# The last four output projections of an adapter moved among self-attention's first units, in one block

## Chip, cores, metric

One Trainium2 chip, one of its cores. The metric is the device time of one execution in microseconds, the median of several runs.

## The reference, cut

Four sequences (B = 4) of 512 tokens of width 160 pass an adapter and then a transformer block. Everything is float32. The adapter:

```python
query = hidden_states @ Wq                       # 8 heads of 20
hs = mha(query, enc @ Wk, enc @ Wv)              # against 73 context rows
ca_q1 = einsum('btc,th->bch', ca, Wq_ca)[:, indices, :]   # 96 rows, repeated to 512
ca_hs1 = mha(ca_q1, residual, residual)
ca_hs2 = mha(ca_hs1 @ Wq, ca @ Wk_ca, ca @ Wv_ca)         # against 4 tokens
out = (hs + ca_hs2) @ Wout + b_out + residual
```

The transformer block (20 heads of 64):

```python
x = cross_attention(layer_norm(x, g1, be1), layer_norm(x, g1, be1), wq1, wk1, wv1, wo1, bo1) + x
x = cross_attention(layer_norm(x, g2, be2), context, wq2, wk2, wv2, wo2, bo2) + x
return geglu_ff(layer_norm(x, g3, be3), w_ff1, b_ff1, w_ff2, b_ff2) + x
```

## The kernel before

Each engine's program is written out by hand in the order in which it is to run, and semaphores join the engines. `adapter` has a block of its own; it ends with a barrier over all engines. `selfattn`, `crossattn` and `feedfwd` then share a second block, each appending to every engine's queue.

**The adapter** works in units u of 128 tokens: NU = 16, four (QT) to a sequence b. Its loop runs over slots s = 0 to 19, and b, k = divmod(s, 4). In slot s TensorE does `scores1(s)` (the 96 token queries against x, two heads), turns the probabilities of s - 1 (L934), projects out unit s - 7 (`project_out`, L1036 and L1037), makes the scores of unit s - 1 (L1004) and turns unit s - 2's (L1014, L1022). VectorE takes maxima (L1222), subtracts (L1233, L1237), sums and inverts (L1241, L1243), empties the last turned piece (`copy_end`, L1250) and adds projections to x (`update`, L1265). ScalarE takes exponentials (L1122, L1127) and copies (L1114, L1134, L1141). POOL scales by the inverses (L1371, L1375), spreads keys and values over blocks (L1340, L1347), adds the bias (`add_bias`, L1354) and makes the rest of self-attention's split weights (L272, L275). Values times the output weights are folded once per sequence at k = 3 (`fold_values`, L986 and L989) and copied by `copy_folded` (L1259), after `inverses` on VectorE. Turned probabilities, projected queries (L909), folded values and the expanded probabilities of the four tokens (`expand_probs2`, L971) all pass through a ring of two PSUM banks, 2 and 3 (`Turns`): an item waits until the item two before it has been copied out.

Self-attention's first LN (`next_ln`, for sequence 0) is made inside the adapter: statistics at s = 14, `standardize` (L157) at s = 15, `turn` (L165, L172) at s = 17, `scale` (L185, L190) and `round` (L202 to L205) on ScalarE at s = 17, `remainder` (L216, L218) on VectorE at s = 18. Units 13 to 15 are projected out after the loop, unit 12 in slot 19.

SP's queue issues all loads; x_t of sequence 1 is the operand of the queries projection in slot 1, x_pad 0 that of `products1` (L946) in slot 3. POOL wants x in slot 3. After the last weight rest SP issues the `last` loads (later weights).

**Self-attention** works on pairs of heads j = 0 to 9 and units u of four per pair. `project_q`, `project_k` (four matmuls, L228 to L231) and `project_v` (L236 to L239) fill a bank; ScalarE rounds it (`round_q` L491, `round_k` L495) and VectorE makes the rest (`rest_q` L561, `rest_k` L566) or copies v (L571). `scores` (L386) fill two banks; VectorE takes maxima (L575), ScalarE exponentials (L503), VectorE inverses (L579), POOL scales (L647); `turns` (L400), copies (L584, L514) and `pv` (L413) follow. Ahead of the loop over sequences a start-up, written out by hand, does the pairs 0 and 1 and units 0 to 5. Batch 0 then begins with `next_v` for pair 2, a turn, and `next_k` for pair 2, which waits for the copy of v:

```python
def next_k(b, j):
    pe.wait_ge(s_vsb.sem, s_vsb.at(b, j))
    project_k(b, j)
```

Before all this each engine increments the semaphores that carry a credit, seven on TensorE. A single bias addition of POOL (`add_bias(0)`, L654) opens its part.

## Time and profile before

| | |
|---|---|
| median of 3 runs | 1015.6 us (1014.93 to 1016.07) |
| the profiled execution | 1019.83 us |
| its span, first to last instruction | 1018.0 us |
| mean granted TensorE clock | 0.993 of full speed |
| busy: TensorE, VectorE, ScalarE, POOL | 974.7, 683.6, 588.9, 377.5 us |
| adapter, start-up, self-attention, rest | 0 to 145, 147 to 163, 163 to 767, 767 to 1018 us |

The profile is one execution. A busy share is an average over stages; what a stage is worth is read from the gaps of the engine that bounds it, each with the instruction that ended it (its releaser). In a timeline row stand start, duration, engine, line, operation, output and inputs, shapes and count, and in brackets the idle time ahead of it with the releaser; "issue" means that nothing in the core released it. Times in the rows are us from the span's start.

### The profile page before, as it was taken

The page shows a single profiled execution, that of the slowest core. Times are in us where ns is not written, and L with a number is a line of the kernel's source. Part 1 is how long each engine was busy: PE and PEld are TensorE (multiplying, and loading weights), DVE is VectorE, ACT ScalarE, POOL GpSimd, SP SyncE. Part 2 cuts the span into 40 slices and gives each one's busy share as a digit, 9 for nine tenths or more (in the row PEclk, how much of TensorE's full clock was granted, in tenths as well). Part 3 has the DMA queues.
Part 4 walks back from the last instruction along what each step waited for, and adds up shares of the span by engine and source line. Part 5 has one row for each costly group of instructions (what it writes and reads, how often), then busy time and mean ns, then how long its engine had stood idle before and what let it go on. Part 6 is the DMA issues. An engine that isn't in the chain of part 4 may idle for free.

```text
span 1018.0 us, 17405 instructions
## 1 busy us (share of the span) xinstructions
PE 974.7 (96%) x6346; PEld 700.8 (69%) x6346; DVE 683.6 (67%) x1164; ACT 588.9 (58%) x1326; POOL 377.5 (37%) x486
## 2 busy tenths in 40 slices
PE   7999989999999999999999999999999989999998
PEld 3566665666567666567666567666566689998887
DVE  3666737776674776674776674776636879999463
ACT  3665636666764666764666764666735455445442
POOL 3576714443332443332444332434311034444120
PEclk9999999999999999999999999999999999999999
DMA  9310230000000000000000000000001330000000
GB/s 268 102 42 2 55 96 1 1 2 1 1 2 1 1 1 2 1 1 1 1 1 1 2 1 2 1 1 1 2 1 36 104 83 1 1 2 1 2 27 26
DMA packets 19585, 22.18 MB, mean 22 GB/s; under 512 B 1366, under 2 KB 17070, under 8 KB 19502
## 3 DMA queue, kind: packets, MB, share of 16 engines
q1 hardware_dynamic: 19502, 21.09, 7.3%
q8 instruction: 51, 0.84, 0.3%
q14 instruction: 32, 0.26, 0.1%
HBM read 15.83 MB, written 1.31 MB: 17 GB/s over the span
## 4 chain that ended last, share of the span: by engine, by line
PE 66%; DVE 10%; ACT 4%; issue 4%; POOL 1%; DMA 0%; SPq 0%; DVEq 0%; ACTq 0%; POOLq 0%
PE banks L413 13%; PE banks L400 12%; PE banks L386 11%; PE banks L420 4%; PE banks L228 3%; ACT sa_probs L503 3%; PE banks L1626 3%; PE banks L229 2%; PE banks L231 2%; PE banks L230 2%; PE banks L1918 2%; DVE ca_top L1761 2%; PE banks L236 2%; DVE ca_probs L1766 2%; DVE sa_negmax L575 1%
## 5 line engine op out<-in xcount | busy, mean ns | idle before, releaser
L647 POOL TENSOR_SCALAR sa_probs<-sa_probs,sa_inverse 128x512 f32<-128x512 f32 x320 | 217.7, 696 | 362.6 <-DVE sa_inverse L579 362.5
L503 ACT ACTIVATE sa_probs<-banks,sa_negmax 128x512 f32<-128x512 f32 x320 | 215.9, 686 | 125.7 <-DVE sa_negmax L575 125.6
L575 DVE TENSOR_REDUCE sa_negmax<-banks 128x2 f32<-128x1024 f32 x160 | 188.7, 1218 | 10.3 <-PE banks L386 7.3
L400 PEld LDWEIGHTS banks<-ident,sa_probs 128*128 128x128 f32 x1280 | 144.4, 140 | 55.6 <-issue 27.6
L400 PE MATMUL banks<-ident,sa_probs 128*128 128x128 f32 x1280 | 172.5, 275 | 10.0 <-ACT sa_turned L514 5.6
L584 DVE COPY sa_turned<-banks 128x512 f32<-128x512 f32 x160 | 110.2, 688 | 75.3 <-PE banks L400 75.3
L413 PE MATMUL banks<-sa_turned,sa_v 128*64 128x512 f32 x640 | 155.0, 605 | 0.0
L386 PE MATMUL banks<-sa_k_parts,sa_q_parts 64*128 64x512 f32 x960 | 133.1, 408 | 1.9 <-ACT sa_probs L503 1.9
L514 ACT COPY sa_turned<-banks 128x512 f32<-128x512 f32 x160 | 94.3, 589 | 58.1 <-PE banks L400 56.3
L386 PEld LDWEIGHTS banks<-sa_k_parts,sa_q_parts 64*128 64x128 f32 x960 | 84.0, 184 | 30.4 <-issue 14.1
L413 PEld LDWEIGHTS banks<-sa_turned,sa_v 128*64 128x64 f32 x640 | 38.7, 136 | 74.2 <-issue 73.0
L1843 POOL TENSOR_TENSOR ca_probs<-ca_probs,ca_inverse 128x770 f32<-128x770 f32 x32 | 48.2, 1509 | 101.4 <-DVE ca_inverse L1772 101.4
L1626 PE MATMUL banks<-fold_values,ca_turned 119*128 119x160 f32 (+1 forms) x416 | 67.2, 307 | 2.2 <-ACT ca_turned L1705 1.5
L579 DVE RECIPROCAL sa_inverse<-sa_total 128x2 f32<-128x2 f32 x160 | 26.1, 163 | 57.7 <-ACT sa_probs L503 57.7
L503 ACT ACTIVATION_READ_ACCUMULATOR sa_probs<-banks,sa_negmax 128x1 f32 x320 | 64.6, 202 | 0.0
L1626 PEld LDWEIGHTS banks<-fold_values,ca_turned 119*128 119x128 f32 (+1 forms) x416 | 60.8, 196 | 3.6 <-issue 2.8
L1695 ACT ACTIVATE ca_probs<-ca_probs 128x770 f32<-128x770 f32 x32 | 27.0, 847 | 35.6 <-DVE ca_probs L1766 35.6
L1705 ACT COPY ca_turned<-banks 119x512 f32<-119x512 f32 x64 | 30.3, 500 | 28.9 <-PE banks L1614 28.9
L420 PEld LDWEIGHTS banks<-w_o,sa_att 128*128 128x128 f32 x320 | 43.6, 190 | 3.2 <-issue 3.2
L571 DVE COPY sa_v<-banks 128x512 f32<-128x512 f32 x40 | 27.6, 691 | 26.4 <-PE banks L239 26.4
L420 PE MATMUL banks<-w_o,sa_att 128*128 128x160 f32 x320 | 44.5, 300 | 0.0
L1614 PE MATMUL banks<-ident,ca_probs 128*119 128x128 f32 (+1 forms) x208 | 33.4, 281 | 4.4 <-POOL ca_probs L1843 3.6
(205 smaller groups left out, 1701.9 us busy)
## 6 DMA issues: line engine op xcount, KB each, us to landing
ad_x_t<-in_x_turned SPq DMA_DIRECT2D x4, 512.0 KB, 5.0
ad_x_pad<-in_x_padded SPq DMA_DIRECT2D x4, 512.0 KB, 8.8
w_o<-in_L_xattn_wo SPq DMA_DIRECT2D x2, 800.0 KB, 9.0
x<-in_x SPq DMA_DIRECT2D x1, 1280.0 KB, 9.1
out<-x SPq DMA_DIRECT2D x4, 320.0 KB, 2.4
w_q_t<-in_L_xattn_wq_t SPq DMA_DIRECT2D x1, 1120.0 KB, 10.6
fold_values<-ca_turned SPq DMA_DIRECT2D x5, 192.5 KB
fold_values<-ca_probs SPq DMA_DIRECT2D x4, 192.5 KB
```

The lines of the kernel that those rows point to most:

```text
L386: last = pe.matmul(bank[:, e, :], q_parts[rows, j % 2, a, q * P:(q + 1) * P], k_parts[rows, j % 2, c, :], start=(i == 0), stop=(i == 2))
L400: last = pe.transpose(b_turn[e][:, q * P:(q + 1) * P], probs[:, j % 2, e, q, k * P:(k + 1) * P], ident[:])
L413: last = pe.matmul(b_out[e * HD:(e + 1) * HD, :], v[:, V_BUF[j // 2], k, c:c + HD], turned[:, u % 2, e, :], start=(k == 0), stop=(k == QT ...
L420: last = pe.matmul(b_turn[q // 2][:, q % 2 * D:(q % 2 + 1) * D], att[:, j, q * P:(q + 1) * P], w_o[:, j, :], start=(j == 0), stop=(j == NP ...
L503: act.activation(probs[:, j % 2, e, q, :], b_scores[u % 2][:, e, :], ACT.Exp, bias=negmax[:, u % RING, e:e + 1], accum_out=total[:, u % RI ...
L514: act.copy(turned[:, u % 2, 1, :], b_turn[1]).then_inc(s_evac_act.sem, 1)
L575: dve.tensor_reduce(negmax[:, u % RING, :], b_scores[u % 2], AX_X, ALU.max, negate=True).then_inc(s_max.sem, 1)
L584: dve.tensor_copy(turned[:, u % 2, 0, :], b_turn[0]).then_inc(s_evac.sem, 1)
L647: pool.tensor_scalar(probs[:, j % 2, e, q, :], probs[:, j % 2, e, q, :], inverse[:, u % RING, e:e + 1], 1.0, ALU.mult, ALU.mult).then_inc( ...
L1614: last = pe.transpose(bank[0:w, n * P:(n + 1) * P], p[:, c:c + w], ident[:])
L1626: last = pe.matmul(b_out[t % 2][:, 0:D], turned[0:w, i, :], folded.values[0:w, t // QT, i, :], start=(i == 0), stop=(i == folded.TILES - 1))
L1843: pool.tensor_tensor(p, p, inverse[:, t % RING, u, :].unsqueeze(2).broadcast_to([P, HH, SK]), ALU.mult).then_inc(s_norm.sem, 1)
```

## The change

Adapter and self-attention share the one block, so the barrier between them is gone; semaphores and PSUM-bank handovers take its place (`AdapterEnd`), and SBUF tiles are allocated in another order so that what self-attention writes first does not lie on what the adapter still reads. The expansion for sequence 3 and the output projections of units 12 to 15, with their updates, become functions that self-attention's start-up calls: the expansion ahead of the first scores, two projections ahead of q of pair 2, two at its end. The start-up's order changes on every engine, and k 0 to q 0 use other banks. In the adapter, the LN turn goes to slot 16, `scale` ahead of the last exponential, `round` and `remainder` to slot 17 in two parts each; `copy_folded` is split around `inverses`, in every sequence; on SP's queue x_t of sequence 1 comes ahead of x_pad 0, and x behind the first weight set. POOL waits for the later biases ahead of its first addition.

```diff
+            adapter_end.weights_split(pe)
             ln.ready(pe, 0)
-            project_q(0, 0, b_proj)
+            project_q(0, 0, b_scores[0][:, 0, :])
             project_k(0, 0, b_out)
+            adapter_end.main_updated(pe)
             project_q(0, 1, b_turn[0])
+            adapter_end.expand_probabilities()
+            scores(0, 0)
             project_k(0, 1, b_turn[1])
-            scores(0, 0)
+            adapter_end.expanded(pe)
             scores(0, 1)
             project_v(0, 0, b_proj)
             pe.wait_ge(s_klo.sem, s_klo.at(0, 0))
             project_v(0, 1, b_out)
             for u in range(2, 2 * LEAD):
                 scores(0, u)
+            pe.wait_ge(s_klo.sem, s_klo.at(0, 1))
+            adapter_end.project_first_half()
             project_q(0, 2, b_turn[0])
             for u in range(2 * LEAD, 2 * LEAD + 2):
                 scores(0, u)
+            adapter_end.project_second_half()
             pe.wait_ge(s_qlo.sem, s_qlo.at(0, 2))
+            adapter_end.updated(pe)
+            adapter_end.later_weights_loaded(pe)
...
-            round_q(0, 0, b_proj)
+            round_q(0, 0, b_scores[0][:, 0, :])
             round_k(0, 0, b_out)
             round_q(0, 1, b_turn[0])
+            adapter_end.copy_expanded()
+            exps(0, 0)
             round_k(0, 1, b_turn[1])
-            exps(0, 0)
             exps(0, 1)
             exps(0, 2)
+            exps(0, 3)
             round_q(0, 2, b_turn[0])
-            exps(0, 3)
...
-            rest_q(0, 0, b_proj)
+            rest_q(0, 0, b_scores[0][:, 0, :])
             rest_k(0, 0, b_out)
             rest_q(0, 1, b_turn[0])
-            rest_k(0, 1, b_turn[1])
             maxima(0, 0)
             maxima(0, 1)
+            rest_k(0, 1, b_turn[1])
+            inverses(0, 0)
             copy_v(0, 0, b_proj)
-            copy_v(0, 1, b_out)
-            inverses(0, 0)
             maxima(0, 2)
             inverses(0, 1)
+            copy_v(0, 1, b_out)
             maxima(0, 3)
+            inverses(0, 2)
+            adapter_end.update_first_half()
+            inverses(0, 3)
             rest_q(0, 2, b_turn[0])
-            inverses(0, 2)
-            inverses(0, 3)
+            adapter_end.update_second_half()
...
+            adapter_end.biases_loaded(pool)
             add_bias(0)
...
+        END = NU - QT
+        out_of = lambda u: b_out[:, OUT:OUT + D] if u < END else banks[5][:, (u - END) % 2 * D:((u - END) % 2 + 1) * D]
...
-        block = ctx.enter_context(nc.Block())
+        end = AdapterEnd(weights_split=lambda eng: eng.wait_ge(s_rest.sem, s_rest.at(len(chunks) - 1, 1)),
+                         main_updated=lambda eng: eng.wait_ge(s_x.sem, s_x.at(END - 1, 0)),
+                         expanded=lambda eng: ring.wait_copied(eng, ("expanded", B - 1, 0)),
+                         updated=lambda eng: eng.wait_ge(s_x.sem, s_x.at(NU - 1, 0)),
+                         biases_loaded=lambda eng: eng.wait_ge(s_later, 16 * len(later)),
+                         later_weights_loaded=lambda eng: eng.wait_ge(s_last, 16 * len(last)))
...
             sp.dma_start(ident[:], t["ident"]).then_inc(s_ident, 16)
+            turned_x(1)
             padded_x(0)
             sp.dma_start(flat(wo[:]), t["wo_padded"]).then_inc(s_wo, 16)
             sp.dma_start(b_o[:], w("b_out").unsqueeze(0).broadcast_to([P, D])).then_inc(s_wo, 16)
             sp.dma_start(expand[:], t["expand"]).then_inc(s_wo, 16)
+            split_weights(0)
             sp.dma_start(x[:], tiles).then_inc(s_x_in, 16)
-            split_weights(0)
-            turned_x(1)
             split_weights(1)
             padded_x(1)
             split_weights(2)
...
-                if 1 <= u < NU - 3:
+                if 1 <= u < END:
                     pe.wait_ge(s_x.sem, s_x.at(u - 1, 0))
-                if u == NU - 1:
-                    pe.wait_ge(s_x.sem, s_x.at(NU - QT, 0))
+                if u >= END + 2:
...
-                if s == NU + 2:
-                    expand_probs2(B - 1)
-                if 0 <= s - OUT_LAG < NU - 3:
+                if 0 <= s - OUT_LAG < END:
                     project_out(s - OUT_LAG)
                 if 0 <= u < NU:
                     scores(u)
+                if s == NU:
+                    pe.wait_ge(s_exp1.sem, s_exp1.at(NU - 1, 1))
+                    next_ln.turn(pe, 0, ident, banks[0:2], lambda i: None)
                 if 0 <= u - 1 < NU:
                     turn_probs(u - 1)
                 if k == 0 and 1 <= b <= B:
...
                     fold_values(b)
                 if k == 3 and b + 1 < B:
                     project_queries(b + 1, 1)
-                if s == NU + 1:
-                    pe.wait_ge(s_exp1.sem, s_exp1.at(NU - 1, 1))
-                    next_ln.turn(pe, 0, ident, banks[0:2], lambda i: None)
-            for u in range(NU - 3, NU):
-                project_out(u)
+
+            def project_first_half():
+                project_out(END)
+                project_out(END + 1)
+
+            def project_second_half():
+                project_out(END + 2)
+                project_out(END + 3)
+
+            end.on_tensor(lambda: expand_probs2(B - 1), project_first_half, project_second_half)
...
+                if s == NU:
+                    act.wait_ge(s_later, 16 * len(later))
+                    next_ln.scale(act, 0, banks[0:2])
+                    exp(NU - 1)
+                if s == NU + 1:
+                    next_ln.round(act, 0, lambda eng: None)
                 if k == 2 and 1 <= b < B:
                     exp2(b - 1)
                 if 1 <= s < NU:
...
                     copy_q2(b - 1)
                 if 0 <= u - 1 < NU:
                     copy_turned(u - 1)
-                if 0 <= u < NU:
+                if 0 <= u < NU - 1:
                     exp(u)
                 if s in chunks:
                     i, c = chunks[s]
...
                     copy_queries(b + 1, 1)
                 if s == NU + 1:
                     exp2(B - 1)
-                    act.wait_ge(s_later, 16 * len(later))
-                    next_ln.scale(act, 0, banks[0:2])
-                    copy_expanded(B - 1)
-                    next_ln.round(act, 0, lambda eng: None)
+            end.on_scalar(lambda: copy_expanded(B - 1))
...
-            def copy_folded(b):
-                if b >= 2:
+            def copy_folded(b, half):
+                if b >= 2 and half == 0:
                     dve.wait_ge(s_o.sem, s_o.at((b - 2) * QT + QT - 1, 0))
-                for half in range(2):
-                    item = ("folded", b, half)
-                    ring.wait_made(dve, item)
-                    n = min(3, CH - 3 * half)
-                    dve.tensor_copy(flat(folded[:, b % 2, 3 * half:3 * half + n, :]), ring.bank(banks, item)[:, 0:n * D]).then_inc(ring.s_dve, 1)
+                item = ("folded", b, half)
+                ring.wait_made(dve, item)
+                n = min(3, CH - 3 * half)
+                dve.tensor_copy(flat(folded[:, b % 2, 3 * half:3 * half + n, :]), ring.bank(banks, item)[:, 0:n * D]).then_inc(ring.s_dve, 1)
 
             def update(u):
                 dve.wait_ge(s_o.sem, s_o.at(u, 0))
...
                     shift2(b - 1)
                 if 1 <= s < NU:
                     max1(s)
+                if s == NU + 1:
+                    next_ln.remainder_main(dve, 0, lambda eng: None)
                 if k == 2 and 1 <= b <= B:
                     finish2(b - 1)
-                if 0 <= s - OUT_LAG < NU - 3:
+                if 0 <= s - OUT_LAG < END:
                     update(s - OUT_LAG)
+                if s == NU + 1:
+                    next_ln.remainder_tail(dve, 0)
                 if 0 <= u < NU:
                     shift(u)
                 if s < NU:
                     inverses1(s)
                 if 0 <= u - 1 < NU:
                     copy_end(u - 1)
+                if k == 3 and b < B:
+                    copy_folded(b, 0)
                 if 0 <= u < NU:
                     inverses(u)
                 if k == 3 and b < B:
-                    copy_folded(b)
+                    copy_folded(b, 1)
                 if s == NU - 2:
                     dve.wait_ge(s_x.sem, s_x.at(QT - 1, 0))
                     next_ln.statistics(dve, 0)
                 if s == NU - 1:
                     next_ln.standardize(dve, 0)
-                if s == NU + 2:
-                    next_ln.remainder(dve, 0, lambda eng: None)
-            for u in range(NU - 3, NU):
-                update(u)
+
+            def update_first_half():
+                dve.wait_ge(s_o.sem, s_o.at(END + 1, 0))
+                update(END)
+                update(END + 1)
+
+            def update_second_half():
+                dve.wait_ge(s_o.sem, s_o.at(END + 3, 0))
+                update(END + 2)
+                update(END + 3)
+
+            end.on_vector(update_first_half, update_second_half)
...
-            adapter(nc, t, x, ident, ctx_t, banks, [(w("wq1"), wa), (w("wk1"), wb), (w("wv1"), wc)], raws, later, last, ln1)
             block = ctx.enter_context(nc.Block())
-            x_ready = selfattn(nc, block, x, ident, ln1, ln2, wa, wb, wc, w_o1, bias["bo1"], banks)
+            end = adapter(nc, block, ctx, t, x, ident, ctx_t, banks, [(w("wq1"), wa), (w("wk1"), wb), (w("wv1"), wc)], raws, later, last, ln1)
+            x_ready = selfattn(nc, block, end, x, ident, ln1, ln2, wa, wb, wc, w_o1, bias["bo1"], banks)
```

## Rows read from the trace of the kernel before

**Rows 1.** The page, busy time of each engine over the span
```profile
PE 974.7 (96%) x6346; PEld 700.8 (69%) x6346; DVE 683.6 (67%) x1164; ACT 588.9 (58%) x1326; POOL 377.5 (37%) x486
```

**Rows 2.** By stretch: busy us (count) of each engine, granted clock, DMA share, GB/s
```profile
22.00:26.00 4.00, 4.00 (x8) 1.16 (x8) 0.00 (x0) 0.47 (x1) 1.82 (x2) 0.57 1.03 240
...
148.00:152.00 4.00, 4.00 (x12) 3.11 (x11) 1.38 (x2) 1.64 (x3) 0.00 (x0) 0.57 0.00 0
...
156.00:160.00 4.00, 3.32 (x19) 1.80 (x18) 3.80 (x7) 3.02 (x9) 2.22 (x4) 1.00 0.00 0
...
170.00:180.00 10.00, 10.00 (x66) 6.40 (x63) 7.20 (x12) 7.98 (x21) 4.07 (x6) 1.00 0.00 0
```

**Rows 3.** Timeline of TensorE in the head: start, us, ..., [idle before <-releaser]
```profile
16.91 1.18 PE L1004 MATMUL banks<-ad_k_diag,ad_q_t 128*128 128x292 f32 x4
21.92 3.58 PE L909 MATMUL banks<-ad_x_t,ad_wq 128*128 128x512 f32 x4 [3.83 <-issue]
...
37.15 1.95 PE L909 MATMUL banks<-ad_x_t,ad_wq 128*128 128x512 f32 x4 [0.86 <-DVE ad_folded L1259]
```

**Rows 4.** Timeline of SP's DMA queue, the issue of x_t of sequence 1
```profile
13.30 0.42 SPq L855 DMA_DIRECT2D ad_x_t<-in_x_turned  x1
```

**Rows 5.** DMA issues at 13.3, 4.7 and 6.6: size, us from issue to landing
```profile
ad_x_t<-in_x_turned SPq DMA_DIRECT2D x1, 512.0 KB, 8.5
...
ad_x_pad<-in_x_padded SPq DMA_DIRECT2D x1, 512.0 KB, 5.4
...
x<-in_x SPq DMA_DIRECT2D x1, 1280.0 KB, 9.1
```

**Rows 6.** Waits of 24 to 125 us: total, times, longest
```profile
PE banks L909 <- DVE ad_folded L1259: 3.2, 3, 1.2
```

**Rows 7.** Timeline of VectorE around the first waits and around one fold
```profile
21.24 0.20 DVE L1243 RECIPROCAL ad_inverse<-ad_total 128x8 f32<-128x8 f32 x1
26.60 1.22 DVE L1222 TENSOR_REDUCE ad_negmax<-banks 96x2 f32<-96x1024 f32 x1 [5.16 <-PE banks L924]
...
93.63 0.76 DVE L1241 TENSOR_REDUCE ad_total<-ad_probs 128x8 f32<-128x584 f32 x1 [0.50 <-ACT ad_probs L1127]
...
94.55 1.01 DVE L1259 COPY ad_folded<-banks 128x480 f32<-128x480 f32 x2
98.35 1.22 DVE L1222 TENSOR_REDUCE ad_negmax<-banks 96x2 f32<-96x1024 f32 x1 [2.78 <-PE banks L924]
```

**Rows 8.** Timeline of TensorE, from slot 16 to the start-up of self-attention
```profile
125.38 0.92 PE L934 MATMUL banks<-ident,ad_probs 96*128 96x96 f32 x8 [1.20 <-DVE ad_folded L1259]
...
147.13 0.47 PE L228 MATMUL banks<-ln_y_hi,wa_hi 128*128 128x512 f32 x1 [2.05 <-issue]
...
147.66 0.39 PE L230 MATMUL banks<-ln_y_hi,wa_lo 128*128 128x512 f32 x1
...
150.02 0.63 PE L229 MATMUL banks<-ln_y_lo,wa_hi 128*128 128x512 f32 x1
```

**Rows 9.** Timelines of VectorE and TensorE, maxima 4 and k of pair 2
```profile
162.30 2.33 DVE L575 TENSOR_REDUCE sa_negmax<-banks 128x2 f32<-128x1024 f32 x2
...
165.85 0.50 PE L228 MATMUL banks<-ln_y_hi,wb_hi 128*128 128x512 f32 x1
```

**Rows 10.** Timelines of VectorE and POOL where both read SBUF at once
```profile
125.55 2.54 DVE L157 TENSOR_SCALAR ln_hat<-x,ln_moments,ln_rstd 128x160 f32<-128x160 f32 x4
...
125.91 1.54 POOL L1354 TENSOR_TENSOR x<-x,ad_b_out 128x640 f32<-128x640 f32 x1
132.11 1.17 POOL L1375 TENSOR_TENSOR ad_probs<-ad_probs,ad_inverse 128x584 f32<-128x584 f32 x1 [4.66 <-DVE ad_inverse L1243]
...
139.83 0.68 DVE L218 TENSOR_TENSOR ln_y_tail<-ln_full_tail,ln_y_tail 32x512 fp32r<-32x512 f32 x1
...
829.63 1.70 POOL L1843 TENSOR_TENSOR ca_probs<-ca_probs,ca_inverse 128x770 f32<-128x770 f32 x1 [5.50 <-DVE ca_inverse L1772]
...
830.03 1.85 DVE L218 TENSOR_TENSOR ca_y_tail<-ln_full_tail,ca_y_tail 32x512 fp32r<-32x512 f32 x1
```

More of the change, by code:

```diff
@@ L788, in adapter @@
         flat = lambda tile: tile.rearrange("p a b -> p (a b)")
-        ring = Turns(ctx, nc, NU, DELTA)
+        ring = Turns(sems, nc, NU, DELTA)
         NK = B * SE
@@ L1392, in _ @@
                     next_ln.deviations(pool, 0)
+        return end
 class Folded:
```

77 lines of the change are left out of this document (47 added, 30 removed).

## The prediction

> **What bounds the kernel now.** I read the page's busy shares first, then the table by stretches, then each engine's timeline at every place where TensorE stands still. TensorE is busy 96% of the span [rows 1]. In self-attention it has no gap at all (170 to 180 us) [rows 2], so a microsecond of TensorE idleness removed ahead of that point moves everything behind it by a microsecond, and any other engine's time counts only where TensorE waits for it. The losses ahead of self-attention's steady state are of three kinds, and the change touches all three.
>
> First, the head. TensorE finishes L1004 near 18.1 and starts the queries projection L909 of batch 1 only at 21.92, after 3.83 us without a releaser inside the core [rows 3]. The operand is x_t of batch 1: its DMA is issued at 13.30, after x's and four of the first weight set [rows 4], and lands 8.5 us later [rows 5], that is at 21.8. Then the same four matmuls take 3.58 us where the later ones take 1.95 [rows 3]; the granted clock of 22 to 26 is 0.57 of full speed, so most of it runs at 1.2 instead of 2.4 GHz [rows 2].
>
> Second, once per batch TensorE waits for folded values: 3.2 us in three waits of up to 1.2, and 1.20 once more at 125.38 [rows 6, 8]. The ring of two PSUM banks must be emptied by L1259, and VectorE does that behind L1241 and L1243, though for a good part of that time it was idle (0.50 us ahead of L1241) [rows 7].
>
> Third, the transition. After the last output projection TensorE stands 2.05 us and starts again at 147.13 [rows 8]. The stretch 148 to 152 has a granted clock of 0.57 [rows 2]; a projection matmul starts every 0.43 us in it, against 0.23 at full clock (compare 150.02 with 147.66) [rows 8]. Then self-attention's first units run as a chain with little else for TensorE to do: 3.32 of 4 us busy between 156 and 160 [rows 2], while VectorE's maxima, ScalarE's exponentials and the copy of v decide when k of pair 2 may be projected, at 165.85 [rows 9]. From there on TensorE is full.
>
> **The change part by part.** *DMA order.* x_t of batch 1 is issued in the place of x_pad 0, at 4.7 instead of 13.3. x_pad 0 landed in the time of its row (5.4 us) [rows 5], so x_t(1) should be there at about 10, far ahead of 18.1. What is moved back: x_pad 0 by one transfer of the same 512 KB (so it lands at 11 to 16, and products 1 want it at 25), and x behind the first weight set, 1.1 MB or about as long as x's own 1.3 MB (it landed at 6.6 + 9.1 = 15.7 [rows 5], so at 25 at the latest; POOL wants it at 34). Both are covered by 9 us. So L909 starts at 18.1 at full clock: 3.8 us of waiting and 3.58 - 1.95 = 1.6 us of slow clock go, 5.4 in sum. What is late next: VectorE ends L1243 of unit 0 at 21.44 [rows 7], while the next maxima would be possible at 26.60 - 5.4 = 21.2. The sum is 5.2 us. From below: if the clock fell anyway, 3.8 less 0.3, 3.5.
>
> *copy_folded in two halves.* The first four fold matmuls of eight (about 1.2 of 2.5 us) are done before VectorE reaches its 0.50 us wait, and the first half's copy (half of 1.01 us) just fits into it [rows 7]. TensorE's next item needs only this half. All three waits vanish: 3.2 us. Behind each wait the other engines are idle and wait for TensorE (VectorE 2.78 us ahead of the next maxima [rows 7], ScalarE and POOL in their timelines more), so nothing is given back. Bounds: 0 (the inverse delayed by as much) to 3.2; I take 3.2, since the copy's slot is idle in the row itself. At slot 16 only 0.3 is gained, because the second ring bank still comes late.
>
> *Transition.* I place the new order on the old times (head and fold gains apart), each instruction with the duration of its like in the timeline of 112 to 172 us. LN's turn goes behind scores 15 (1.0 us, at 128.2: the standardized tile is there at 128.1, and not earlier, since its second instruction ends with POOL's bias addition [rows 10]). ScalarE now runs both scale steps (0.67 each) ahead of exp 15, which so starts at 130.25 against 130.31: free, because the shifted scores come no sooner. The rounding, three casts of 0.6, stands ahead of copy_q2, which is 0.9 us later than before; TensorE fills this with output projection 10. TensorE idles 1.0 us (hs1) as before, scores2 come at 134.9, output projection 11 could start at 135.55 when copy_end 15 is through, and self-attention's first projection after 1.4 us more, at 136.95. TensorE's seven semaphore increments lie between; where crossattn begins inside a block TensorE shows no gap for the same thing, so zero.
>
> Into this falls a new meeting. `remainder_main` (two SBUF inputs) can start at 132.3, in the middle of POOL's L1375 (132.1 to 133.3) [rows 10], behind which POOL now adds self-attention's bias at once (1.5 us; in the old kernel it ran alone at 145.75). The trace shows what such a meeting costs: L218, 0.68 us at 139.83 beside an idle POOL, took 1.85 us at 830.03 beside POOL's L1843, and ended half a microsecond after it [rows 10]. Behind it in VectorE's queue stand update 10, remainder_tail and copy_end 15, on which projection 11 waits. If VectorE gets in between the two POOL instructions, remainder_tail is held until 136.0 and TensorE loses 0.75 us; if POOL's addition goes first, 1.1; if they do not meet, nothing. I take 0.9 and start self-attention at 137.85.
>
> The Trainium skill, page "SBUF — State Buffer", section "SBUF: two separate sides", says that VectorE with two SBUF inputs and GpSimd hold one port pair exclusively, for a whole instruction. By that rule the sum loses the 0.75 to 1.1 us, without it nothing; the trace agrees with the rule at 830 us.
>
> From 137.85 TensorE has work without a gap: q 0 (0.93), k 0 (0.93), q 1 (0.93), the expansion (0.95, its probabilities ready at 137.8), scores 0 (0.8; its k rest is ready at 141.3), k 1, scores 1, v 0 and v 1 (0.96 each), scores 2 and 3, projections 12 and 13 (1.37 each), q 2, scores 4 and 5, projections 14 and 15. Scores 2 and 3 wait at most 0.3 us for exponentials, since now VectorE takes unit 0's maxima before k 1's rest. The last projection ends near 156.0. Then a **new wait**: batch 0 may begin only when VectorE has written the update of 14 and 15 (two of 0.33), so TensorE idles 0.8 us until 156.8. What is queued behind that update on VectorE is maxima 4, whose scores have been ready since 152.6. From the start of maxima 4 to k of pair 2 the old trace takes 165.85 - 162.30 = 3.55 us [rows 9], and the order of that piece is unchanged; TensorE spends it on v 2 and one turn (2.0 us) and idles for the rest. So k of pair 2 stands at 156.75 + 3.45 = 160.2 instead of 165.85: a gain of 5.65 us. What disappears is the 2.05 us of handover, ten matmuls at 0.43 instead of 0.23 (2.0), and part of the start-up's waits, which the 5.4 us of projections now fill. Bounds: 6.5 (no meeting) and 2.9 (the clock falls again, below). The later weight loads end long before their new wait (landed by 137; it stands at 156).
>
> Sum: 5.2 + 3.2 + 5.65 = 14.05 us. The profiled execution took 1019.8 (span 1018.0), 4.2 above the median of 1015.6; the gains are of waits, not of that offset, so they come off the median: **1001.5 us**. A measurement of this kernel tells about 0.2% (2 us) from no change.
>
> **The rivals.** *A, the head's gain does not come:* some transfer other than x_t(1) is late at 18 to 25, or the clock still falls. For: the DMA engines are full until 34 us. Against: the landing row hits the wait's end to 0.1 us. 1015.6 - 8.85 = 1006.7, or 1003.2 with the clock alone. *B, the fold split only shifts the wait* to VectorE's inverses and POOL behind them: 1004.7. For: the copy's fit is exact to 0.1 us; against: the reserves above. *C, the transition falls to half clock:* TensorE idles 1.0 + 0.4 + 1.4 us between 130.7 and 136.5, or 0.8 + 1.4 between 156 and 160. A gap of 2.05 us preceded the old fall, the gap of 1.20 at 125.38 did not lead to one [rows 8]. A fall costs up to 1.8 us for what ten matmuls lost at 150, and in both places 2.8: 1003.3 to 1004.3. *D, slower than before:* the merged order leaves TensorE so sparse that it stays at half clock through the whole stretch from 126 to the steady state, and VectorE's in-order queue (update halves ahead of maxima) feeds it too late to recover. At half clock a full microsecond of work costs another one; it needs more than 14 us lost, that is 14 us of full-clock work and the waits between done at 1.2 GHz, almost all of the 17 us of work from 137.85 to 156, on top of C's place. Against: the old fall ended after 4 us. 1017 or more. *E, the barrier was free:* its 2.05 us is the time of the same increments and first weight loads; then the transition gives 3.6 and the time is 1003.5.
>
> **How the numbers follow.** Forecast 0.60; A 0.11; B 0.09; C 0.11; E 0.05; D 0.03; the rest 0.01 (near no change). The forecast's own range is 999.5 (no meeting, and one of the start-up waits of about 1 us gone) to 1003 (half of the fold's gain missing). The range for 8 in 10 takes in B, C and E and most of A, and reaches 1.5 us below the forecast's own, since the gap of 1.4 us on the copy of v and the 0.8 us ahead of it may turn out shorter than laid out: 998.0 to 1006.0. Faster by over 0.2% in all cases but D and the rest: faster 0.96, within 0.2% 0.01, slower 0.03.
>
> **What would show each step.** L909 of batch 1 near 18.1 with 1.95 us and a clock of 1.00 in 18 to 26 (head); no TensorE gap with L1259 as releaser in the slots 4, 8 and 12 (fold); a remainder_main or remainder_tail of over 1 us beside POOL (meeting); no clock below 1.00 between the first projection and k of pair 2, and a gap of about 0.8 us on the update of 15, then about 1.4 us on the copy of v (transition). From 170 us on every piece should keep its length. The prediction is wrong if self-attention's batches change in length, or if TensorE's gaps reappear between 18 and 34 us with a DMA behind them.

## The result, and the profile after

The changed kernel took 1007.1 us in the median of 4 executions (1006.35 to 1007.99), the kernel before 1015.7 (1014.93 to 1016.07): a ratio of 0.992 with a 95% interval of 0.990 to 0.993. That is 8.65 us faster, not the 14.05 of the forecast, and outside its range of 998 to 1006. The profiled execution took 1007.99 us.

The page of after, its span, TensorE's busy time and the granted clock in 40 slices (compare [rows 1]):

```profile
span 1005.9 us, 17398 instructions
PE 973.7 (97%) x6346; PEld 698.3 (69%) x6346; DVE 685.2 (68%) x1164; ACT 588.8 (59%) x1326; POOL 376.9 (37%) x486
PEclk8999999999999999999999999999999999999999
```

TensorE does the same work in a shorter span. The one 8 in the clock's row is its first slice, the head. After by stretch there and at the transition (columns as in [rows 2]):

```profile
12.00:16.00 4.00, 4.00 (x6) 1.51 (x5) 1.78 (x4) 1.44 (x4) 2.25 (x6) 0.50 1.04 290
...
148.00:152.00 4.00, 4.00 (x30) 3.36 (x28) 0.69 (x1) 0.19 (x1) 1.23 (x2) 1.00 0.00 0
```

From 12 to 16 the granted clock is 0.50, the lower of its two levels (1.2 GHz), although TensorE is busy all the time; from 148 to 152, where [rows 2] has 0.57, it is now full. TensorE in the head, first in before, then in after, which answers to [rows 3]:

```profile
10.54 3.70 PE L909 MATMUL banks<-ad_x_t,ad_wq 128*128 128x512 f32 x8
...
25.43 1.13 PE L924 MATMUL banks<-ad_x_t,ad_q 32*96 32x512 f32 x4
```

```profile
12.45 6.25 PE L959 MATMUL banks<-ad_x_t,ad_wq 128*128 128x512 f32 x8
...
22.39 1.88 PE L959 MATMUL banks<-ad_x_t,ad_wq 128*128 128x512 f32 x4
24.20 1.10 PE L974 MATMUL banks<-ad_x_t,ad_q 32*96 32x512 f32 x4
```

The wait of 3.83 us and the slow 3.58 are gone, as forecast. But the projection of batch 1 begins at 22.39, not near 18.1: the eight matmuls of batch 0 take 6.25 us, where they took 3.70 at 10.54 in the profiled execution of before. The head has lost its wait and has a low clock instead. The transfers came as laid out: x_t of batch 1 was there at 10.5 us and x at 22.0.

The fold in after, VectorE and then TensorE (compare [rows 7, 8]):

```profile
118.63 0.64 DVE L1317 COPY ad_folded<-banks 128x480 f32<-128x480 f32 x1
119.21 0.76 DVE L1300 TENSOR_REDUCE ad_total<-ad_probs 128x8 f32<-128x584 f32 x1
...
120.12 0.44 DVE L1317 COPY ad_folded<-banks 128x320 f32<-128x320 f32 x1
...
120.71 0.52 PE L984 MATMUL banks<-ident,ad_probs 96*128 96x96 f32 x4 [0.54 <-DVE ad_folded L1317]
```

The first half's copy stands ahead of the reduction. TensorE's waits at slots 4, 8 and 12 are gone; at slot 16 there are 0.54 us left of 1.20. VectorE in before, then VectorE and POOL in after, ahead of the first projection of self-attention (compare [rows 10]):

```profile
139.12 0.68 DVE L216 TENSOR_TENSOR ln_y_lo<-ln_full,ln_y_hi 128x512 fp32r<-128x512 f32 x1
```

```profile
127.59 1.16 POOL L1447 TENSOR_TENSOR ad_probs<-ad_probs,ad_inverse 128x584 f32<-128x584 f32 x1 [4.63 <-DVE ad_inverse L1302]
127.70 1.60 DVE L220 TENSOR_TENSOR ln_y_lo<-ln_full,ln_y_hi 128x512 fp32r<-128x512 f32 x1 [0.20 <-ACT ln_y_hi L202]
128.71 1.99 POOL L678 TENSOR_TENSOR x<-x,bo 128x640 f32<-128x640 f32 x1
130.12 1.12 DVE L226 TENSOR_TENSOR ln_y_tail<-ln_full_tail,ln_y_tail 32x512 fp32r<-32x512 f32 x1
```

The forecast meeting is there, twice: VectorE's two subtractions took 1.60 and 1.12 us beside POOL, and 0.68 each in before, where POOL was idle. By the rows the first of the two costs TensorE nothing: behind it VectorE waits 0.46 us for TensorE before it can do update 10 (129.76). The start-up of self-attention, TensorE and VectorE (compare [rows 8, 9]):

```profile
132.99 0.50 PE L240 MATMUL banks<-ln_y_hi,wa_hi 128*128 128x512 f32 x1
...
146.35 0.51 PE L240 MATMUL banks<-ln_y_hi,wa_hi 128*128 128x512 f32 x1
147.49 1.66 PE L398 MATMUL banks<-sa_k_parts,sa_q_parts 64*128 64x512 f32 x12
...
152.09 0.56 DVE L1323 TENSOR_TENSOR x<-banks,x 128x160 f32<-128x160 f32 x2 [3.18 <-PE banks L1087]
152.57 2.35 DVE L597 TENSOR_REDUCE sa_negmax<-banks 128x2 f32<-128x1024 f32 x2
152.75 0.35 PE L248 MATMUL banks<-wc_hi,ln_y_hi 128*128 128x256 f32 x1 [0.70 <-issue]
...
155.38 0.69 DVE L593 COPY sa_v<-banks 128x512 f32<-128x512 f32 x1
156.12 0.50 PE L240 MATMUL banks<-ln_y_hi,wb_hi 128*128 128x512 f32 x1 [1.29 <-DVE sa_v L593]
```

No handover gap and no fall of the clock; the new wait behind the update is 0.70 us and the one on the copy of v 1.29. VectorE stood 3.18 us ahead of the update with maxima 4 and 5 queued behind it.

### The profile page after: what moved, and what is told of

It is laid out like the page before. It is cut to its first block, busy times and chain, and to the rows that moved or that the text cites. A ratio compares the mean times of both kernels' runs of the same rounds, so it can differ in the third digit from the quotient of the medians.

```text
span 1005.9 us, 17398 instructions
## 1 busy us (share of the span) xinstructions
PE 973.7 (97%) x6346; PEld 698.3 (69%) x6346; DVE 685.2 (68%) x1164; ACT 588.8 (59%) x1326; POOL 376.9 (37%) x486
## 4 chain that ended last, share of the span: by engine, by line
PE 78%; DVE 11%; issue 4%; ACT 4%; POOL 1%; DMA 0%; SPq 0%; DVEq 0%; ACTq 0%; POOLq 0%
PE banks L425 13%; PE banks L412 12%; PE banks L398 12%; PE banks L432 4%; PE banks L240 3%; PE banks L243 2%; PE banks L241 2%; PE banks L242 2%; PE banks L1700 2%; PE banks L1992 2%; ACT sa_probs L524 2%; PE banks L1086 2%; PE banks L248 2%; DVE ca_top L1835 2%; PE banks L959 2%
## 5 line engine op out<-in xcount | busy, mean ns | idle before, releaser
L1700 PE MATMUL banks<-fold_values,ca_turned 119*128 119x160 f32 (+1 forms) x416 | 64.6, 299 | 2.0 <-ACT ca_turned L1779 1.4
L1700 PEld LDWEIGHTS banks<-fold_values,ca_turned 119*128 119x128 f32 (+1 forms) x416 | 58.3, 190 | 3.5 <-issue 2.6
L240 PE MATMUL banks<-ln_y_hi,wb_hi 128*128 128x512 f32 x80 | 36.5, 456 | 1.3 <-DVE sa_v L593 1.3
```

The costliest lines, as they stand in the source:

```text
L240: pe.matmul(bank, w.hi[:, c], self.hi[:], start=True, stop=False)
L1700: last = pe.matmul(b_out[t % 2][:, 0:D], turned[0:w, i, :], folded.values[0:w, t // QT, i, :], start=(i == 0), stop=(i == folded.TILES - 1))
```

## The experiments

In the expectations T3 is the theory that the head's low clock covers the landing of x_t(1). Executions of one kernel differ by where the granted clock falls, so the mean clock of an execution is given where it tells something. "The second unit of scores1 of batch 1" is the matmul group (L924, in after L974) right behind the queries projection of batch 1; its start says what the head cost.

**Both kernels once more.** The profile that the forecast rests on took 1019.8 us, 4.2 above its kernel's median. Is it like the others?

> The kernel before, unchanged, for a second profiled execution and for the spread of its runs. Theory T1 (the offset of 4.2 us between the first profile, 1019.83, and its median is two falls of TensorE's clock at 820 and 940 us that most executions do not have): the new profile has a span near 1014 and no fall, or one, behind 764 us. Theory T2 (profiling itself costs 4 us in this kernel): again a profiled execution near 1019.8 with the same four stretches of low clock. In both the queries projection of sequence 1 starts at 21.9 us, since x_t's landing sets it, whether TensorE's clock was low or high between 10 and 18 us.

> The changed kernel, unchanged. If the half clock between 10.6 and 18 us of its first profile was chance (rival), the runs are in two groups 4.4 us apart, or the new profile shows 1.00 there and the queries projection of sequence 1 at 18.1 instead of 22.4. If it comes in nearly every execution of this program (theory), the profile shows it again and all runs lie within 2 us of 1007.

The kernel before: 1015.7 us in 12 executions. Its new profile, by stretch, and TensorE behind it:

```profile
8.00:12.00 4.00, 4.00 (x19) 2.08 (x17) 0.86 (x2) 0.81 (x1) 0.16 (x1) 0.85 1.03 292
12.00:16.00 4.00, 4.00 (x6) 1.51 (x5) 1.77 (x4) 1.44 (x4) 2.24 (x6) 0.50 1.13 388
16.00:20.00 4.00, 4.00 (x11) 1.87 (x11) 0.00 (x0) 1.47 (x3) 0.91 (x2) 0.80 1.04 208
...
21.37 1.18 PE L1004 MATMUL banks<-ad_k_diag,ad_q_t 128*128 128x292 f32 x4
22.56 1.96 PE L909 MATMUL banks<-ad_x_t,ad_wq 128*128 128x512 f32 x4
24.45 1.10 PE L924 MATMUL banks<-ad_x_t,ad_q 32*96 32x512 f32 x4
```

No idle time is shown ahead of the queries of batch 1, though both theories expected their start at 21.9. The clock is low from 10.8 to 17.6 us, and TensorE comes to them at 22.56, as late as the transfer: it was issued at 13.83 and landed 8.6 us later, at 22.4. In after, with the transfer there since 10.5, the same place is reached at 22.39, so at most 0.2 us of a wait was left. The profiles of before_dma and before_fold below have the low stretch too (0.50 from 12 to 16). The wait of [rows 3] belongs to an execution whose head ran at full clock.

The offset of a profile from its median is another matter. This one took 1018.7 us, again 3.0 above its median, and like the first it has the clock low at 820 and 940 us (0.61 from 820 to 824, 0.67 from 940 to 944). The profiles of before_dma, before_fold and before_dense have neither fall, and take 3.6 us less from k of pair 2 to the end (848.6 against 852.2). So T1's falls are real but came twice; and since those three profiles lie at or under their medians, it is not profiling that costs 4 us (T2).

The changed kernel took 1007.4 to 1009.1 us in five executions, with a mean clock of 0.993 or 0.995, and 1002.8 in one with 1.00. That one was profiled:

```profile
10.50 3.70 PE L959 MATMUL banks<-ad_x_t,ad_wq 128*128 128x512 f32 x8
...
17.88 1.88 PE L959 MATMUL banks<-ad_x_t,ad_wq 128*128 128x512 f32 x4
19.69 1.10 PE L974 MATMUL banks<-ad_x_t,ad_q 32*96 32x512 f32 x4
```

Here the queries of batch 1 start at 17.88 with no wait, near the 18.1 of the forecast. So the forecast described an execution that came once in the ten of after.

The head's price can now be read at either level of the clock, with no work added. At full clock the second unit of scores1 of batch 1 came at 25.43 in before and at 19.69 in after_again: 5.74 us. At the low one it came at 24.45 in before_again and at 24.20 in after: 0.25 us.

Since the profiles of before_again and of after have the same low stretch in the head, their difference can be split by places: the second unit of scores1 of batch 1, the unit of slot 15, and k of pair 2, first in before_again, then in after (its k of pair 2, at 156.12, stands above).

```profile
115.21 1.10 PE L924 MATMUL banks<-ad_x_t,ad_q 32*96 32x512 f32 x4
...
164.77 0.50 PE L228 MATMUL banks<-ln_y_hi,wb_hi 128*128 128x512 f32 x1 [0.16 <-DVE sa_v L571]
```

```profile
111.62 1.10 PE L974 MATMUL banks<-ad_x_t,ad_q 32*96 32x512 f32 x4
```

So the head gave 0.25 us, the folds (115.21 - 24.45) - (111.62 - 24.20) = 3.34, the transition (164.77 - 115.21) - (156.12 - 111.62) = 5.06, 8.65 in all. That the medians differ by 8.65 as well is partly luck: behind k of pair 2 the two profiles differ by another 2.4 us (852.2 against 849.8), because the clock falls at 820 and 940 in before_again and at 724 in after (0.57 from 724 to 728), and the new executions of both kernels give medians 7.9 apart.

**One part alone.** The kernel before with the new order of transfers, and with the split copy.

```diff
+            turned_x(1)
             padded_x(0)
...
-            sp.dma_start(x[:], tiles).then_inc(s_x_in, 16)
             split_weights(0)
-            turned_x(1)
+            sp.dma_start(x[:], tiles).then_inc(s_x_in, 16)
```

> The kernel before with the new DMA order alone (x_t of sequence 1 ahead of x_pad 0, x behind the first weight set). By the prediction: 5.2 us faster, 1010.5. By the theory that TensorE works at half clock between 10.6 and 18 us once nothing stops it there, and that the transfer's landing at 21.8 us had hidden this: 0.8 to 1.2 us faster, 1014.6, and the profile shows 0.5 to 0.6 of full clock from 11 to 18 us.

1015.3 us, a ratio of 0.999 (0.997 to 1.000). Ten of 11 executions took 1014.6 to 1015.9 with a mean clock of 0.995, one 1010.15 with 1.00. Its profile, at low clock, has the second unit of scores1 of batch 1 here:

```profile
23.71 1.10 PE L924 MATMUL banks<-ad_x_t,ad_q 32*96 32x512 f32 x4
```

That is 0.74 us earlier than in before_again, and TensorE was 0.48 us ahead already at the scores before the queries (L1004 at 20.89 against 21.37), so 0.26 us of it can be the order's. Between the medians its worth can't be told from nothing. The rare execution lies 5.2 us below its median; not all of that is the head's, since a mean clock of 1.00 leaves no room for the fall at 148 us either.

```diff
+                if k == 3 and b < B:
+                    copy_folded(b, 0)
                 if 0 <= u < NU:
                     inverses(u)
                 if k == 3 and b < B:
-                    copy_folded(b)
+                    copy_folded(b, 1)
```

> The kernel before with copy_folded split around the inverses in every sequence, nothing else. By the prediction three waits of 0.86, 1.19 and 1.20 us go and 0.3 us at slot 16: 1015.6 - 3.5 = 1012.1. The rival, that the wait is only moved to the inverses: no change. The first profile of the changed kernel showed 3.66 us gained at these places.

1010.7 us, 0.995 (0.994 to 0.997). TensorE's waits for the copies, first in before_again, then in before_fold:

```profile
PE banks L909 <- DVE ad_folded L1259: 3.4, 3, 1.2
PE banks L934 <- DVE ad_folded L1259: 1.2, 1, 1.2
```

```profile
PE banks L934 <- DVE ad_folded L1258: 0.5, 1, 0.5
```

From the second unit of batch 1 to k of pair 2 the profiles give (164.77 - 24.45) - (160.06 - 23.47) = 3.73 us, 3.42 of them in the three folds. Of the remaining 1.25 us of the measured 5, 0.98 lies ahead of the first fold (24.45 against 23.47), where nothing was changed: there the clock was back at full 1.6 us earlier.

**The clock of the head.** If the low clock hides the gain, keeping it up must bring out both the old wait and the new order's worth. Two dense matmuls are added, their output is not used:

```diff
             last.then_inc(s_q1p.sem, 1)
+            dense(1)
             pe.wait_ge(s_w, 32)
             for g in range(G):
+                if g == 1:
+                    dense(1)
```

where `dense(1)` is one 128x512 matmul of ones into bank 3.

> Added to the kernel before: two dense 128x512 matmuls (0.93 us each at 2.4 GHz) with nothing of their output used, one behind the four-row matmuls of q1 and one between the two groups of the keys, where TensorE's work is small. Theory T3 (the head's clock falls to 1.2 GHz from about 10.6 to 17.5 us in most executions, at 3.4 us of cost, and covers the landing of batch 1's turned x): the clock stays at 2.4 GHz there, TensorE comes to queries(1) at about 20 instead of 22.4, the wait for x_t(1) is seen again (2 to 4 us ahead of the line of project_queries), the second unit of scores1 of batch 1 starts at 24.4 to 25.4 as before, and the time is 1015.5 to 1017 us. Rival (the clock of the head follows no work of the kernel): the half clock stays, 1.9 to 2.8 us are added: 1018 to 1019. Rival (the landing is not what limits): 1013.5 to 1014.

> The same two dense matmuls, added to the kernel before with the new order of transfers. T3: no half clock from 10.6 to 17.5, no wait for x_t(1), the second unit of scores1 of batch 1 at about 21.6 instead of 23.7, and 2.1 to 2.4 us off the 1015.3 of the new order alone: 1012.9 to 1013.5; so the new order of transfers is then worth 3 to 4 us where it is worth 0.4 to 0.7 with the clock low. Rival (the clock follows nothing of the kernel): 1017 to 1018, and no more between the two orders than before.

> The same two dense matmuls, added to the changed kernel. T3: head at 2.4 GHz from about 7 us on, scores1's second unit of batch 1 at 21.6 instead of 24.2, and 2.2 to 2.6 us off 1007.8: 1005.2 to 1005.6. Rival: 1009.5 to 1010.5.

The kernel before with them: 1015.2 us, 0.9995 (0.998 to 1.001). Its head by stretch and on TensorE:

```profile
12.00:16.00 4.00, 4.00 (x11) 1.58 (x12) 2.64 (x6) 1.70 (x5) 1.96 (x5) 1.00 1.12 386
...
19.30 1.18 PE L1004 MATMUL banks<-ad_k_diag,ad_q_t 128*128 128x292 f32 x4
21.66 1.96 PE L909 MATMUL banks<-ad_x_t,ad_wq 128*128 128x512 f32 x4 [1.19 <-issue]
```

With the new order of transfers as well, 1012.6 us, 0.998 (0.996 to 0.999):

```profile
20.57 1.88 PE L909 MATMUL banks<-ad_x_t,ad_wq 128*128 128x512 f32 x4
```

The clock stays full and the wait is back (1.19 us, ended at 21.66, the landing again; less than the 2 to 4 us expected), and the order of transfers takes it away: the second unit of scores1 of batch 1 starts at 23.55 without the new order and at 22.39 with it, 1.16 us (3 to 4 us were expected). Together with the two pairs of profiles above (0.25 us at low clock, 5.74 at full clock with no work added) that shows the cover: low clock and late transfer run beside each other, and only the removal of both pays.

The medians say less. They lie 2.7 us apart with the dense matmuls and 0.4 without, but executions of before_dma_dense run from 1011.2 to 1019.0 us, and only 1.16 us of the 2.7 stands in the head. Four of its 12 executions (1011.2 to 1011.5) have a mean clock of 1.00, so no fall at 148 us, and none of the 11 of before_dense has; why is open.

The changed kernel with them took 1007.8 (1004.0 to 1008.3, 5 executions), two at 1004.0 and 1004.8 with a mean clock of 1.00, three near 1008 with 0.997; the median did not move, so the expected 1005.2 to 1005.6 was not met. Where the clock of the long ones fell is open; in the profile of before_dma_dense, a long one too (1015.4 us), the head is at full clock and it falls later, to 0.67 from 108 to 112 us and 0.71 from 148 to 152.

Without added work, the third warming matmul moved behind q1:

```diff
-            keep_busy(WARM)
+            keep_busy(WARM - 1)
...
             last.then_inc(s_q1p.sem, 1)
+            dense(1)
```

> The changed kernel with no matmul added: the third of the three warming ones is moved from ahead of q1 to behind it. T3, if one dense matmul there is enough: head at 2.4 GHz, scores1's second unit of batch 1 at 19.7 to 20.7, and 3.4 to 4.2 us off 1007.8: 1003.6 to 1004.4. If one is not enough, or the rival holds: 1007 to 1008.5, the half clock between 9 and 18 still there.

> The kernel with the third warming matmul behind q1 once more, for the profile of one of its long executions (4 of 9 took 1010.6 to 1011.8 with a mean clock of 0.998; 5 took 1002.4 to 1003.3). If two warming matmuls leave TensorE at half speed all through the small matmuls of the head, the profile of a long one shows 0.46 us and more a pass of 512 columns in places up to 16 us and later. Rival: the head is the same and the 8 us lie at a wait for a transfer later on.

The first time 5 of 9 executions took 1002.4 to 1003.3 and 4 took 1010.6 to 1011.8, the second time all four 1003.4 to 1006.2: medians of 1003.3 and 1004.5, so here the head's gain does reach the median (after: 1007.1 and 1007.8), at the price of a long kind that after does not have. An execution that is long in the head was caught by the profile of after_best below, which has the same head. First TensorE in after_moved (1002.4 us), then in after_best (1005.9 us):

```profile
6.39 1.13 PE L1096 MATMUL banks<-ad_turned 128*128 128x512 f32 x2
```

```profile
5.26 2.92 PE L1109 MATMUL banks<-ad_tokens,ad_wq_ca 4*128 4x384 f32 x4
8.12 2.08 PE L1103 MATMUL banks<-ad_turned 128*128 128x512 f32 x2
...
13.59 2.02 PE L981 MATMUL banks<-ad_x_t,ad_q 32*96 32x512 f32 x4
15.54 4.88 PE L966 MATMUL banks<-ad_x_t,ad_wq 128*128 128x512 f32 x8
```

In after_best the same matmul takes 2.08 us instead of 1.13, and everything up to about 18 us is at half speed: the engine had never come out of the slow state it starts in. The mean clock of that execution reads 1.00. So with two warming matmuls ahead of q1 an execution can go through the whole head without getting warm. Whether the four executions of 1011 us were this and nothing more was not seen.

**The order in the start-up.** Maxima ahead of the update on VectorE, and TensorE's wait moved behind the projection of v:

```diff
             rest_q(0, 2, b_turn[0])
+            for u in range(2 * LEAD, 2 * LEAD + 2):
+                maxima(0, u)
             adapter_end.update_second_half()
...
+                    if b == 0 and d == 0:
+                        adapter_end.updated(pe)
                     turns(b, 2 * d)
```

> The changed kernel with two orders of the new stretch altered: the maxima of units 4 and 5 of self-attention are taken ahead of the update of tiles 14 and 15 on VectorE, and TensorE waits for that update only ahead of the first turn into bank 5, behind the projection of v of pair 2. If the chain of the new stretch is (update of 14 and 15, maxima 4 and 5, copy of v, k of pair 2), as the trace of after reads: the projection of k of pair 2 comes 1.5 to 2.1 us earlier against the first projection of self-attention (23.1 us in after), and the time is 1.5 to 2.0 us under 1007.8. Rival (the wait is only shifted to the exponentials behind the maxima, ScalarE's turn copies then come last): 0 to 0.7 us.

1004.1 us (1000.1 to 1004.7), 0.989 (0.988 to 0.991). VectorE and TensorE:

```profile
144.26 2.35 DVE L598 TENSOR_REDUCE sa_negmax<-banks 128x2 f32<-128x1024 f32 x2
...
147.52 0.56 DVE L1329 TENSOR_TENSOR x<-banks,x 128x160 f32<-128x160 f32 x2 [0.91 <-PE banks L1093]
...
148.47 0.69 DVE L594 COPY sa_v<-banks 128x512 f32<-128x512 f32 x1 [0.33 <-PE banks L251]
149.22 0.50 PE L240 MATMUL banks<-ln_y_hi,wb_hi 128*128 128x512 f32 x1
```

From the first projection (128.45) to k of pair 2 it is 20.77 us, in after 156.12 - 132.99 = 23.13: 2.36 us less, and both of TensorE's waits are gone. The two waits together were 1.99 us, so the repair is worth a little more than they were.

The medians differ by 3.7 us, more than the rows give. Executions with the same mean clock differ by 2.3 (1006.4 and 1004.1 at 0.997) and 2.7 (1002.8 and 1000.1 at 1.00). The rest of the 3.7 is one more fall of the clock: most executions of after read 0.995 or less, as its profile with the fall at 724 us does and that of after_bias_late with one at 928, and none of the four of after_order reads below 0.996. Whether the new order takes that fall away was not shown.

**The meeting of VectorE and POOL.** POOL's addition waits until the tail is made:

```diff
             adapter_end.biases_loaded(pool)
+            pool.wait_ge(ln.s_lo.sem, ln.s_lo.at(ln.before, 1))
             add_bias(0)
```

> The changed kernel with GpSimd's add of the output bias to batch 0 (128x640, 1.99 us at 128.71) held back until VectorE has made the tail of the remainder. If the meeting of the two engines is what stretched the tail's subtraction to 1.12 us and held the copy of the turned end behind it: the tail takes 0.5 to 0.6 us, the output projection of tile 13 and self-attention's first projection come 0.6 us earlier against the projection of hs1, and the time falls by 0.4 to 0.7 us; the main remainder (1.60 us beside the scaling of the probabilities) stays as it is. Rival (VectorE's form is that slow by itself): no change.

1007.8 us (1007.1 to 1009.0), level with after_again's 1007.8: half a microsecond is too little for four executions. The trace tells it:

```profile
130.03 0.68 DVE L226 TENSOR_TENSOR ln_y_tail<-ln_full_tail,ln_y_tail 32x512 fp32r<-32x512 f32 x1
130.85 1.54 POOL L678 TENSOR_TENSOR x<-x,bo 128x640 f32<-128x640 f32 x1 [2.18 <-issue]
...
132.46 0.50 PE L240 MATMUL banks<-ln_y_hi,wa_hi 128*128 128x512 f32 x1
```

The tail takes 0.68 instead of 1.12, POOL's addition 1.54 instead of 1.99, and the first projection comes 0.53 us earlier (0.08 of that lies ahead of the main subtraction, which is unchanged at 1.60). So the meeting cost TensorE 0.45 us.

**All together.**

> The changed kernel with the two dense matmuls in the head, the order of maxima and update, and the late bias. The runs of the dense head alone gave 1004.0 to 1004.8 where the clock never fell and 1007.8 to 1008.3 where it did. If the parts add up: 2.0 to 2.6 us less, 1001.4 to 1002.8 with no fall, 1005.2 to 1006.3 with falls.

> The changed kernel with the order of maxima and update and with the late bias, the head as it is. By the two traces of these parts (2.4 and 0.5 us): 1007.8 less 2.7 to 3.2, so 1004.6 to 1005.1 where the head's clock is low (mean clock 0.995 to 0.996), and 1000 where it is not. Rival (the parts overlap, since both shorten the way to the first turns): 1005.5 to 1006.

> The same with the third warming matmul moved behind q1. If the head's clock is what hides the gain of the new order of transfers: 3.5 to 4.5 us less than after_order_bias in most executions, 999.8 to 1001.3. Rival (a fall saved in the head comes back as a fall elsewhere, or the long executions come again): 1003 or more in the median, with single executions of 1007 and above.

after_all 1003.4 us (1002.2 to 1004.8; 0.9885), after_order_bias 1004.0 (999.9 to 1004.3; 0.987), after_best 1003.0 (1000.0 to 1009.1; 0.987). The two repairs of the start-up give 3.9 us between the medians on top of the change, and 2.4 (at 0.997) to 2.9 (at 1.00) between executions of the same mean clock. In after_order_bias five of six executions took 1003.5 to 1004.3 with a mean clock of 0.997, and the profiled one of them has its head at low clock; the sixth took 999.9 with 1.00. The difference of 4 us is the head's share (second unit of scores1 of batch 1 at 23.47 in this profile, at 19.65 in that of after_order). On top of the repairs no edit of the head brought more than 1 us of it into the median: three executions of after_best took 1000.0 to 1000.2, as expected, the other three 1005.9 to 1009.1; the first of these is the one seen above, the other two have no profile. The version to keep is after_order_bias; by its interval it lies 1.1 to 1.5% below the kernel before.

## Why the prediction was wrong, point by point

**Head: forecast 5.2 us, came 0.25.** This is the step that failed, and 4.95 of the 5.4 us missed. What the forecast read in [rows 3 to 5] was right for that execution: the queries of batch 1 waited for the landing. What it did not ask is whether the executions that make the median have this wait. By three of the four profiles of the kernel before and its two one-part variants (before_again, before_dma, before_fold) they don't: their head is at 1.2 GHz until 16 to 17.6 us and reaches the place when the transfer lands. Where the head does run at full clock the forecast holds, 5.74 us against 5.2. The forecast set the profile's 4.2 us above the median aside as an offset that has nothing to do with waits; by the second profile about 1 us of it (25.43 against 24.45) was the wait that was priced, and most of the rest the falls at 820 and 940. Two dense matmuls brought the wait back, at 1.19 us. Rival A named the right result (1006.7) for a near reason, that the clock is low; it had a chance of 0.11, and the low clock that it meant was the one of 22 to 26, not of 10 to 18. The range was also drawn too tight by its own rivals: it was said to take in most of A, but A's main price of 1006.7 lies above its end of 1006.0, and that is where the time fell.

**Fold: forecast 3.2, came 3.3 to 3.4**, and the 0.3 at slot 16 as well. Rival B is out: with the split alone the time fell by 5.0 us, 3.42 of it in the three folds.

**Transition: forecast 5.65, came 5.1** (5.2 against the first profile of before: 165.85 - 116.12 less 156.12 - 111.62). The barrier's gap and the fall of the clock at 148 went, and no profile of the changed kernel or its variants has a fall between 30 and 170 us, so rivals C, D and E are out. The waits of 0.8 and 1.4 us measured 0.70 and 1.29. The meeting is real, but it cost 0.45 us by the late bias and not 0.9: only the tail's 0.44 us was on TensorE's way, and by the rows the 0.92 us of the main subtraction was not. Laid on the old times (4.50 us added at slot 15), the first projection came at 137.5 against the forecast 137.85. What was too small, and outweighed this, is the stretch of dense work behind it: to the end of the last projection 19.1 us against 18.15. TensorE has no gap there; the matmuls of each kind were priced by their steady rows, and where one kind follows another they take 0.1 to 0.2 us longer, as q of pair 2 at 146.35 (1.14 us to the next kind, priced 0.93). Behind k of pair 2 the length was kept: in the profiles without a late fall it is 848.6 us to the end with the old start-up and 848.7 to 849.4 with the new.

**The base.** To take gains off the median and not off the profiled time was right for the folds and the transition, as far as the fall at 148 is in the executions that make the median. It was not right for a gain that exists only in the profiled execution.

**What the forecast did not price** is the order of update and maxima: the 0.8 us were listed as a new wait, with maxima 4 queued behind it. By the forecast's own layout the scores for maxima 4 were ready at 152.6 and the update came at 156; turning the two round was worth 2.4 us.

The Trainium skill, page "SBUF — State Buffer", section "SBUF: two separate sides", says that a VectorE instruction with two SBUF inputs and a GpSimd instruction that reads SBUF lock each other out; the forecast weighed this rule. The late bias is a direct test for the tail, and the trace agrees: 0.68 us alone, 1.12 beside POOL. Both subtractions in after ended 0.54 to 0.55 us behind the end of the POOL instruction that they met (129.30 behind 128.75, 131.24 behind 130.70).

## What to carry to other kernels

Before a wait is priced from one profile, ask whether the executions that make the median have it; a second profile of the unchanged kernel is the cheapest experiment there is. The distance of a profile from its median did not tell: both profiles of before lay 3 to 4 us above the median, and only one had the wait. A low clock and a late transfer in one stretch cover each other, so neither is worth its own length; compare both orders at both levels of the clock, in rows of the stretch itself, since medians also hold falls of the clock elsewhere. Compare executions of the same mean clock before a repair is given the whole difference of two medians. Where two engines' queues are merged, put what the critical engine's next bank waits for ahead of updates that nobody needs soon (2.4 us here), and keep additions of bulk data on POOL away from a VectorE subtraction that TensorE waits for (0.45 us here).

## What the runs showed of the hardware

The granted clock fell to 1.2 GHz in the head although TensorE's row was busy for all of 8 to 16 us; what it had run just before were four-row matmuls (1.7 us) and 96-row matmuls of 16 and 292 columns (2 us). The same matmuls do not always end so. Nine profiles have this head with nothing added: in the three where the three warming matmuls took 4.5 to 4.6 us (before, after_again, after_order) the clock stayed at 2.4 GHz up to 20 us, in the six where they took 4.9 to 5.5 us it fell. With two dense matmuls put among the small ones it stayed at 2.4 GHz in all four profiles, though the warming took 5.2 to 5.5 us in three of them.

The way out of the slow start differs from one execution of the same kernel to the next: the three warming matmuls of after took 4.5 us in one profile and 5.5 in another. The Trainium skill, page "TensorE: Matmul & The Clock Gate", section "Part 1: The HAM clock gate (the "warmup" mystery)", says that the number of slow matmuls at the start varies from run to run; the traces agree. What they add is its price here, 4.5 us in the head between two executions of the changed kernel (24.20 against 19.69), and that the granted clock reads 1.00 while matmuls at the start take twice their time (2.08 against 1.13 us): there the durations must be read, not the clock.
